# A decoder of two layers on one core: one skip term, the front stage's last rounds, the token list of the experts, and the first three heads' keys

## The reference, cut to what matters

```python
x = LN(x + diff_attention(x))                 # front stage
x = LN(x + long_conv(v=x, x1=ctx, x2=ctx))    # conv stage, middle stage
x = LN(x + moe(x))                            # 8 experts, 2 for each token
x = LN(x + attention(x))                      # tail: "P"
x = LN(x + cross_attention(x, ctx))           # tail: "C"
x = LN(x + shared_kv_attention(x))            # tail: "H" and "A"

# long_conv: kv = v_i * x2_j in groups of 8 rows (i, j in the group)
y = conv(kv, filter) + kv * skip;  out_j = sum_i y_ij * x1_i
# moe: top 2 of 8 logits, each token goes to two experts
# shared_kv_attention, 16 heads of 32:
gating = softmax(x @ W_gate.T);  idx = argmax(gating)
k_shared = one_hot(idx) . k      # one head's keys for each token
v_shared = one_hot(idx) * max(gating) . v
```

## Time and profile before

| | |
|---|---|
| median of 3 runs | 2275.7 us (2269.55 to 2280.37) |
| the profiled execution's own time, its span | 2275.38 us, 2273.6 us |
| granted TensorE clock, mean | 0.966 |
| PE busy, DVE busy | 2116.7 us (93%), 1231.6 us (54%) |
| ACT busy, POOL busy | 517.4 us (23%), 589.0 us (26%) |
| on the chain that ended last | PE 37%, DVE 5%, ACT 1%, POOL 1% of the span |

### The profile page before, as it was taken

How to read it: one execution, slowest core, us unless ns; L and a number is a source line. 1 busy time by engine, 2 the same in 40 slices (tenths; PEclk the granted TensorE clock), 3 DMA queues, 4 the chain that set the end, 5 groups by cost and what they waited for, 6 DMA issues and landing times. The chain is left out here.

```text
span 2273.6 us, 29273 instructions
## 1 busy us (share of the span) xinstructions
PE 2116.7 (93%) x11864; PEld 1231.1 (54%) x11872; DVE 1231.6 (54%) x1861; ACT 517.4 (23%) x783; POOL 589.0 (26%) x544
## 2 busy tenths in 40 slices
PE   6899999888999899799999878999999999999996
PEld 4444444233444476456666646566666666666653
DVE  2467777667999841022222234355757575747456
ACT  1444444430000121111111112122222222222221
POOL 1122222227888405011110311212121212111112
PEclk9999999989999899899999989999999999999997
DMA  9840000005111146811221510101010101000000
GB/s 174 96 40 29 29 29 19 31 19 191 41 46 41 51 152 113 230 65 66 67 67 61 205 69 29 47 1 47 1 56 1 57 1 38 3 27 10 1 10 19
DMA packets 66762, 129.63 MB, mean 57 GB/s; under 512 B 7450, under 2 KB 20968, under 8 KB 66632
## 3 DMA queue, kind: packets, MB, share of 16 engines
q1 hardware_dynamic: 44952, 75.43, 13.1%
q10 hardware_dynamic: 14976, 33.69, 5.3%
q0 software_dynamic: 6704, 18.64, 2.8%
HBM read 96.38 MB, written 41.85 MB: 61 GB/s over the span
## 5 line engine op out<-in xcount | busy, mean ns | idle before, releaser
L925 PE MATMUL conv_conv<-kv,toep 128*128 128x512 f32 x576 | 248.9, 595 | 4.6 <-POOL kv L946 4.6
L2223 DVE RECIPROCAL tail_inv<-tail_ring 128x256 f32<-128x256 f32 x64 | 112.4, 1756 | 181.6 <-PE tail_ring L1691 181.4
L1393 PE MATMUL moe_gu_ps<-gu,moe_xT 128*128 x624 | 199.6, 463 | 3.4 <-issue 1.8
L925 PEld LDWEIGHTS conv_conv<-kv,toep 128*128 128x128 f32 x576 | 110.0, 191 | 144.2 <-issue 136.1
L946 POOL TENSOR_TENSOR kv<-vT,cT 128x512 f32<-128x512 f32 x128 | 160.5, 1275 | 48.7 <-PE conv_conv L925 38.9
L1393 PEld LDWEIGHTS moe_gu_ps<-gu,moe_xT 128*128 128x128 f32 x624 | 116.3, 192 | 72.8 <-issue 23.6
L1968 POOL TENSOR_TENSOR tail_rstd_x<-tail_rstd_x,const_minus_half 128x2 f32<-128x2 f32 x32 | 22.6, 707 | 482.1 <-DVE tail_rstd_x L2175 482.1
L1975 POOL TENSOR_SCALAR_AFFINE_SELECT tail_expT<-tail_expT 128x1024 f32<-128x1024 f32 x64 | 70.4, 1100 | 288.6 <-ACT tail_expT L2045 288.1
L540 POOL TENSOR_SCALAR_AFFINE_SELECT front_expT<-front_expT 128x2048 f32<-128x2048 f32 x32 | 64.4, 2012 | 259.8 <-ACT front_expT L598 259.8
L1475 DVE TENSOR_TENSOR moe_hid<-moe_gu_ps,moe_silu 128x352 f32<-128x352 f32 x39 | 20.5, 525 | 179.4 <-PE moe_gu_ps L1393 179.4
L2045 ACT ACTIVATE tail_expT<-tail_scores 128x1536 f32<-128x1536 f32 x64 | 92.8, 1451 | 76.4 <-PE tail_scores L1669 76.4
(11 more groups left out here) (335 smaller groups left out, 4035.7 us busy)
## 6 DMA issues: line engine op xcount, KB each, us to landing
toep<-toeplitz SPq DMA_DIRECT2D x32, 320.0 KB, 2.8
y_slots<-moe_y ACTq DMA_DIRECT2D x39, 256.0 KB, 2.0
gu<-in_L_ffn_gate_up_proj SPq DMA_DIRECT2D x5, 1408.0 KB, 10.5
toeplitz<-filt_rows SPq DMA_DIRECT2D x1, 6144.0 KB, 67.2
front_e<-in_ctx SPq DMA_DIRECT2D x8, 512.0 KB, 5.6
toeplitz<-filt_rows SPq DMA_DIRECT2D x2, 2048.0 KB, 89.9
x_after<-x SPq DMA_DIRECT2D x8, 512.0 KB, 5.1
tail_x<-x_after SPq DMA_DIRECT2D x8, 512.0 KB, 3.8
```

What stands on the lines that cost most here:

```text
L925: ins = pe.matmul(bank, toep[p][:, mat * P:(mat + 1) * P], kv[p][:, c].rearrange("p b j i -> p (b j i)"), start=n == 0, stop=n == len(PART ...
L1393: ins = pe.matmul(gu_ps[:, s % 2, h, 0:HID], xT[:, c, :], wgu[c][:, e, h * HID:(h + 1) * HID], start=c == 0, stop=c == NC - 1)
L2223: link.after(dve.reciprocal(inv[c % 2][:], bank[:, S:2 * S]))
```

## The change

- **Skip term of the last sequence.** In the front stage, `skip_products(7)` writes into the buffer `e[2]`, which is free by then, and that stage ends after it, without `octets(7)`, `add_skip(7)` and the store of batch 7. These become the first work of the conv stage on PE, DVE and SP. The wait for `base_stored` stays where it was on ACT.
- **Order of the front stage's end.** In round 10, PE takes `turn_context(7)`, `weigh(7, 1, 1)` and `square_sums(7, 0)` ahead of `turn_tokens(6)`; ACT takes the context, the sums and the root ahead of the tokens.
- **One-hot token list.** DVE makes, for each token's two slots, a one-hot row of its lane in the tile (`at_lane`, 128 wide, bf16) and its tile marked with the row number and the block number (`marked`, 2 x 39, bf16). 32 bf16 matmuls sum them into one bank; DVE adds block * 128 + row. They stand after b = 2 of the context loop. The 32 indirect DMAs, the clearing of `token_of`, its load and its transpose go. SP issues the second half of the weights when the bank is filled.
- **End of the middle stage.** The wait for `ctx_q` and `ctx_o` moves from ACT's end of the middle stage to the top of ACT's list in the experts stage, ahead of the load of `wq`.
- **Gates with three heads' keys.** `wgate` and `gk` lie side by side in one tensor. The gates' products have 16 + 96 = 112 columns (for both t), the keys' products 416 columns instead of 512. `gate_choice` copies 2 x 112 columns out of PSUM instead of 2 x 16; `pick("k")` is two products instead of one: 96 columns from SBUF and 416 from PSUM. `wgate` is loaded with the other H weights, later than before.

```diff
@@ front stage, PE
                     elif f is not None:
-                        turn_tokens(u)
                         turn_context(f)
                         weigh(f, 1, 1)
                         square_sums(f, 0)
+                        turn_tokens(u)
                         square_sums(f, 1)
                         octets(u)
...
                     elif u is not None:
                         turn_tokens(u)
-                        octets(u)
@@ front stage, SP and DVE
-                for b in range(B):
+                for b in range(B - 1):
                     sp.wait_ge(based, b + 1)
...
-                    if u is not None: skip_products(u)
+                    if u is not None: skip_products(u, skipped if u < B - 1 else e[last_skip])
...
-                    if u is not None: add_skip(u)
+                    if u is not None and u < B - 1: add_skip(u)
@@ conv stage, PE, SP, DVE: ahead of their loops
+                for t in range(NT):
+                    bank = ring.claim(pe, ("oct", t))
+                    pe.matmul(bank, consts["octets"][:], skipped[:, t, :], start=True, stop=True).then_inc(ring.filled_sem(("oct", t)), 1)
...
+                sp.wait_ge(based, 1)
+                sp.dma_start(base.rearrange("(b t p) d -> b p t d", p=P, t=NT)[B - 1], x_last).then_inc(mid.base_stored[(B - 1) % 5], 16)
...
+                for t in range(NT):
+                    key = ("oct", t)
+                    dve.wait_ge(ring.filled_sem(key), ring.count(key))
+                    dve.tensor_tensor(skipped[:, t, :], ring.tile(key), e_last[:, t, :], ALU.mult).then_inc(ring.drained_sem(key), 1)
...
+                dve.tensor_tensor(x_last, x_last, skipped[:], ALU.add).then_inc(based, 1)
@@ middle stage, PE
                 for b in range(1, B - 2):
                     ctx_queries(b)
                     ctx_values(b)
-                pe.wait_ge(rows_loaded, 16)
-                bank = ring.claim(pe, "tokens")
-                pe.transpose(bank[:, 0:TILES], token_rows[:], consts["ident"][0:TILES, 0:TILES]).then_inc(ring.filled_sem("tokens"), 1)
+                    if b == 2:
+                        pe.wait_ge(hot_ready, 1)
+                        bank = ring.claim(pe, "tokens")
+                        for t in range(T):
+                            for n in range(PICKS):
+                                ins = pe.matmul(bank[:, 0:2 * TILES], at_lane[:, t, n], marked[:, t, n].rearrange("p a s -> p (a s)"),
+                                                start=t + n == 0, stop=t + n == T + PICKS - 2)
+                        ins.then_inc(ring.filled_sem("tokens"), 1)
@@ middle stage, SP and POOL
-                sp.wait_ge(placed, 16 * T * PICKS)
-                sp.dma_start(token_rows[:], token_of.rearrange("(a p) o -> a (p o)", p=P)).then_inc(rows_loaded, 16)
+                sp.wait_ge(ring.filled_sem("tokens"), ring.count("tokens"))
...
-                for t in range(T):
-                    for n in range(PICKS):
-                        pool.indirect_dma_start(
-                            out=token_of, out_offset=bass.IndirectOffsetOnAxis(ap=slot[:, t, n:n + 1], axis=0),
-                            in_=ids[:, t:t + 1], in_offset=None).then_inc(placed, 16)
@@ middle stage, DVE, behind tile_expert
+                dve.wait_ge(stored[NX - 1], 16 * len(range(NX - 1, B, NX)))
+                link.after(dve.tensor_tensor(reached[:], over(slot_f[:], TILES + 1), over_picks(bounds[:], TILES + 1), ALU.is_ge))
+                link.after(dve.tensor_reduce(tile_of[:], reached[:, :, :, 1:TILES + 1], AX_X, ALU.add))
+                link.after(dve.scalar_tensor_tensor(out=lane_of[:], in0=tile_of[:], scalar=-float(P), in1=slot_f[:], op0=ALU.mult, op1=ALU.add))
+                dve.tensor_tensor(at_lane[:], over(lane_of[:], P), over_picks(lanes[:], P), ALU.is_equal)
+                link.after(dve.tensor_tensor(in_tile[:], reached[:, :, :, 0:TILES], reached[:, :, :, 1:TILES + 1], ALU.subtract))
+                dve.tensor_scalar(marked[:, :, :, 0], in_tile[:], row_id[:, 0:1], None, ALU.mult)
+                dve.tensor_tensor(marked[:, :, :, 1], in_tile[:], block_id[:].unsqueeze(2).unsqueeze(3).to_broadcast([P, T, PICKS, TILES]),
+                                  ALU.mult).then_inc(hot_ready, 1)
@@ ACT: end of the middle stage, top of the experts stage
-                for p in range(2):
-                    act.wait_ge(ctx_stored[p], 32 * ((B - 2) // 2))
...
+                for p in range(2):
+                    act.wait_ge(mid.ctx_stored[p], 32 * ((B - 2) // 2))
                 for k in early:
@@ tail, PE (the eight calls of rows("H", "k", ...) become shared_keys)
+                    n = NG + LED * HD
+                    for t in range(NT):
+                        ins = project_rows(pe, bank[:, t * n:(t + 1) * n], xT[b % 2], t, wide["gk"], 0, n)
...
+                def shared_keys(b, t):
+                    bank = ring.claim(pe, ("H", "k", b, t))
+                    project_rows(pe, bank[:, 0:D - LED * HD], xT[b % 2], t, wide["gk"], NG + LED * HD,
+                                 NG + D).then_inc(ring.filled_sem(("H", "k", b, t)), 1)
@@ tail, DVE, pick("k")
-                        ins = dve.tensor_tensor(chosen, bank, of, ALU.mult)
+                        dve.tensor_tensor(chosen[:, 0:LED], led[:, t].rearrange("p (h d) -> p h d", d=HD), of(0, LED), ALU.mult)
+                        ins = dve.tensor_tensor(chosen[:, LED:NG], bank[:, 0:NG - LED], of(LED, NG), ALU.mult)
```

More of the change, by code:

```diff
@@ L632, in _ @@
                             take(("turn", d, n), pair(xT, n))
-                    if a is None and u is not None:
-                        for n in range(2):
-                            take(("x1", u, n), vT[:, 2 * n:2 * n + 2, u, :])
                     if a is None and f is not None:
@@ L640, in _ @@
                     if f is not None: root(f, 0)
+                    if a is None and u is not None:
+                        for n in range(2):
+                            take(("x1", u, n), vT[:, 2 * n:2 * n + 2, u, :])
                     if d is not None: take_query(d, 0)
@@ L856, in __init__ @@
         self.base_stored = [st.sem(f"base_stored{p}") for p in range(5)]
+        self.ctx_stored = [st.sem(f"ctx_stored{p}") for p in range(2)]
         self.gathered = [st.sem(f"gathered{p}") for p in range(2)]
@@ L967, in _ @@
                 link = Link(dve, linked, 1 << 30)
+                for t in range(NT):
[3 more added lines that the diff above has]
+                for t in range(NT):
+                    key = ("oct", t)
+                    dve.wait_ge(ring.drained_sem(key), ring.count(key))
+                dve.tensor_tensor(x_last, x_last, skipped[:], ALU.add).then_inc(based, 1)
                 def sums(h, lc):
@@ L986, in _, with middle_stage @@
                         sums(h, lc)
-def middle_stage(nc, consts, mid, region, base, x_out, vT, cT, w_router, w_gu, w_down, wa, wvo, ctx_q, ctx_o, token_of, slot, share):
+def middle_stage(nc, consts, mid, region, base, x_out, vT, cT, w_router, w_gu, w_down, wa, wvo, ctx_q, ctx_o, slot, share):
     T = B * NT
@@ L1037, in middle_stage @@
         stored = [st.sem(f"stored{p}") for p in range(NX)]
-        ctx_stored = [st.sem(f"ctx_stored{p}") for p in range(2)]
         router_loaded = st.sem("router_loaded")
@@ L1536, in tail_stage @@
         descending = st.sb("descending", [P, NG])
-        gate, gex, ranked, ind = (st.sb(n, [P, NT, NG]) for n in ("gate", "gex", "ranked", "ind"))
+        gated = allowed[:, 2, 0:NT * (NG + LED * HD)].rearrange("p (t n) -> p t n", t=NT)
+        gate, led = gated[:, :, 0:NG], gated[:, :, NG:NG + LED * HD]
+        gex, ranked, ind = (st.sb(n, [P, NT, NG]) for n in ("gex", "ranked", "ind"))
         gtop, first, gsum, gval = (st.sb(n, [P, NT]) for n in ("gtop", "first", "gsum", "gval"))
@@ L1813, in _ @@
                     if A_: shared_out(a)
-                    if H_: turned("H", h); rows("H", "k", h, 0, xT[h % 2], wide["gk"]); gates(h)
+                    if H_: turned("H", h); shared_keys(h, 0); gates(h)
                     if r == 0:
@@ L1848, in _ @@
                 score("A", a, 1)
-                rows("H", "k", h, 0, xT[h % 2], wide["gk"])
+                shared_keys(h, 0)
                 score("A", a, 2)
@@ L1854, in _ @@
                 rows("C", "v", c, 1, xT[c % 2], wvo)
-                rows("H", "k", h, 1, xT[h % 2], wide["gk"])
+                shared_keys(h, 1)
                 shift("A", a)
@@ L1927, in _ @@
                 load("wo")
-                load("wgate")
                 for b in range(2):
@@ L1933, in _ @@
                 sp.wait_ge(ring.filled_sem(key), ring.count(key))
-                for k in ("gk", "gv", "gq"):
+                for k in ("wgate", "gk", "gv", "gq"):
                     load(k)
@@ L2237, in gate_choice @@
                     key = ("H", "g", b)
```

(9 more changed lines are left out.)

89 lines of the change are left out of this document (50 added, 39 removed).

## The result

| | before | after |
|---|---|---|
| median of the runs, us | 2275.5 (2269.55 to 2280.37, n = 4) | 2248.94 (2246.92 to 2251.49, n = 4) |
| ratio, 95% interval | | 0.9881 [0.9859, 0.9902] |
| profiled execution, us (span) | 2275.38 (2273.6) | 2249.93 (2248.1) |

Forecast 2256.5 (2247 to 2266), measured 2248.94: 26.6 us saved where the working found 19.2. The time lies in the range, outside the likeliest case's own 2251 to 2261. The issues that open the stages say where the two profiled spans part. Each column is the length of a stretch in us, ended by the row named.

What follows compares the result with a forecast made beforehand. It took TensorE alone to pace the tail, and TensorE and VectorE both to be full in conv. Savings of 1.5 + 8.2 + 9.5 = 19.2 us from the median of 2275.7 gave 2256.5 us, range 2247 to 2266.

Steps and rivals of the forecast that it cites:

- likeliest case: Whole kernel: the forecast as it stands, 15 to 24 us saved, so 2251 to 2261 us; chance 0.68.
- Front, order of round 10: End of the front stage: weigh starts 2.8 us sooner, ACT's token copies give 1.2 back; about 1.5 us saved.
- Seam to conv: Front to conv: the stage starts 5.1 us sooner, but its first both comes 5.1 us later from there.
- this lasts to the end: Conv stage: the 5.1 us delay of the first both stays, since DVE's following 243 us are full.
- Rival 1: Conv stage: the late store costs more, PE gets no free bank, 7.8 us more delay, 2264 us; chance 0.12.
- Rival 2: Conv stage: DVE catches up as L985 waits less, 4.5 us more saved, 2252 us; chance 0.10.
- rival 4: Conv stage: POOL locks L985 at its dear end, 28 us added, 2284 us, slower than before; chance 0.04.
- Middle: End of the middle stage: the experts start at 934.5 instead of 942.68, 8.2 us saved.
- SP's weights are gone by 910 or so: Middle stage: SP's second half of the weights starts at about 891 and is gone by 910 or so.
- Tail: Tail: shorter key products save 1.26 us a sequence, six rounds 7.5 and the last two sequences 2.0; 9.5 us saved.
- Rival 3: Tail: the gates' 112 columns come on top of the weight loads, the key change does nothing, 2266 us; chance 0.06.
- The lock that the prediction weighed: Tail picks: with two SBUF inputs a pick may wait for one POOL instruction, 0.9 us; the sum stays.

Runs made afterwards that it cites:

- e2: The kernel before with the new order of round 10 alone (token turns and copies moved later); 2292.73 us, ratio 0.9996 to the kernel before.
- e1: The kernel before with the skip term of batch 7 made in the conv stage, nothing else; 2291.3 us, ratio 0.9991 to the kernel before.
- e3: The kernel before with the one-hot token list and the moved wait for the context stores alone; 2267.48 us, ratio 0.9883 to the kernel before.
- e6: The changed kernel with ACT's waits for the stores of base, its x loads and first gu load moved behind its copy for h = 3; 2245.35 us.
- e10: The changed kernel with 14 unused products of 512 columns added behind PE's last product of the conv stage; 2254.43 us.
- e4: The kernel before with the gates' 96 shared key columns alone; 2284.25 us, ratio 0.9955 to the kernel before.
- e8: The changed kernel with ACT's wait for the context stores back at the end of the middle stage, the one-hot list kept; 2256.06 us.
- e7: The changed kernel with four heads' keys in the gates' products (144 columns) instead of three (112); 2247.17 us.
- e9: The changed kernel with all 512 key columns multiplied again, the gates still 112 columns wide and their 96 key columns unused; 2257.71 us.
- e12: The changed kernel with e6's late loads, e7's four heads, and batch 7's octets, their DVE work and store of base behind h = 0 of conv; 2249.06 us.

## Why the prediction was nearly right, point by point

**Front, order of round 10: 1.5 forecast, 2.9 measured** (e2, and e1 against the kernels with both). Its two steps were right: `weigh` starts 2.6 us sooner (forecast 2.8), and ACT's token copies give 0.9 back (1.2), since from the first square sum to the second it is now 6.08 us instead of 5.13. At one clock in `weigh` that makes 1.6 us at the second square sum, e2 against e3. Missing is the clock, 1.3 us in `weigh`; the forecast priced this stretch at one level.

**Seam to conv: 5.1 saved, 5.1 lost; measured 5.4 saved and 6.1 lost.** The mechanism was right as far as `both`: the store of `base` and ACT's wait for it, for e6 without the wait has `both` 8.4 us behind the start. Three sizes were off, and they nearly cancel, which is luck. The landing took 9.2 us for 4 to 5, the loads behind it 2.0 for 3.7, so `both` came 8.5 us later than before and not 5.1. And "this lasts to the end" was wrong by 2.4 us, which DVE made up (next point). Rival 1 didn't come: PE ran its 576 products without a gap, in 248.6 us (before 248.9). Rival 2 came in part, 2.4 of its 4.5 us, by its own mechanism.

**L985's spread, rival 4.** It didn't decide, but it is real. The line's mean was 1168 ns before, 1131 after, and 1113 to 1144 in six of the others and 804 to 825 in six, never in between:

```profile
L1001 DVE TENSOR_TENSOR prod<-total,cT x64: 692/882/1514, 533.6 to 772.2; 128x512 f32<-128x512 f32 x64
```

```profile
L1002 DVE TENSOR_TENSOR prod<-total,cT x64: 691/693/1611, 527.2 to 769.2; 128x512 f32<-128x512 f32 x64
```

(One line's ns, min/median/max, first of the changed kernel, then of e6.) In windows 640:680 DVE is busy 38.93 us of 40 in the first state and 36.08 in the second. In the first, dear state DVE sets the stage's end. From its first `total` to SP's load of `wr` it takes 243.88 us before and 241.49 after; without the line's own 64 products (74.8 and 72.4 us) that is 169.1 in both, and in five more of the eight profiles in that state (all but e10, whose added products end its stage). So the late `both` goes through to the end, less what the line gives: 8.5 us late, 2.4 given back, 6.1 longer. In the second, cheap state PE sets the end: in all six profiles the stage ends 2.8 to 2.9 us behind its last product.

No run has the late `both` in the cheap state. By estimate it would cost nothing there, since 169.1 + 52.8 = 222 us of DVE's work would fit behind it; and an early `both` in the dear state would end at 10.1 + 241.5 = 251.6 us, before PE's 255. e6 changed both at once, so its 3 to 5 us may be put down to either. In the kernel before the dear state cost 1.1 us: 254.05, and 252.98 in e4, with the cheap one, the same code in this stage and the same 248.9 us of PE's stream.

The Trainium skill, "SBUF — State Buffer", "Who interferes with whom", names what may be the reason, a shared port pair that VectorE and GpSimd lock against each other. The rows fit it, but no run took GpSimd's work away. That there are two states, and nothing between, is what these rows add; what chooses the state is open.

**Middle: 8.2 forecast, 9.0 measured.** The one-hot products took 1.34 us instead of 2.0, and nothing else was off in size. The reasons were mixed, though. "SP's weights are gone by 910 or so" is nearly right of the loads issued by 891, which land by 913, but one load waits for the last context values and goes at 926. The moved wait carries 6.7 of the 9.0 (e8), the list 2.3. In the group of e1 to e4 the list carries some 17 more (25.9 for the whole edit).

**Tail: 9.5 forecast, 11.9 measured.** Rounds: 1.26 forecast, 1.21 measured, as priced by the line through two widths; a third width (e7) and the free columns (e9: 0.08 us) agree. Rival 3 is out. The missing term is the clock: the last two sequences gave 5.1 us instead of 2.0, some 2.6 of it the clock by the estimate above. Behind wide gates the key product took 3.06 instead of 4.57 us, where its 96 columns fewer are worth 0.6. The lock that the prediction weighed against this change shows in 2 of 16 picks: the new product of 96 columns with both inputs in SBUF took 251 to 260 ns fourteen times and 1066 and 1266 ns twice, so it was no term of the sum.

**Chance.** 2.7 us at the middle's start came by no edit.

Added up for the profiled pair: front and seam 0.7 more than forecast (8.3 - 6.1 = 2.2 against 1.5), middle 0.8, its clock 2.7, tail 2.4, less 0.2 in the experts: 6.4 us on top of 19.2, and 25.6 stands beside the spans' 25.5. The medians lie 26.6 apart; the last microsecond is within their spread.

What stays open: what the scatters of four-byte rows block in one group of runs and not in another, and whether they alone explain why the kernel before takes 2299 us in the third group, where no profile has them; what puts L985 in one state or the other; and why one of four kernels with the old order kept its clock in round 10.

## What to carry to other kernels

Where TensorE's weight loads set the pace, columns added to those products are nearly free up to the load's time (0.08 us for 96 columns in 16 gates), and shorten another product at full price (1.2 us a round): look for narrow products that share their weights with a wide one. A wait that only protects a later reader belongs behind the first work that doesn't need it: here two waits of ACT, for stores in DRAM, were worth 6.7 us of a stretch (the context stores, moved by the change) and 3 to 5 us of a stage, 2.6 by the medians (the store of `base`, which the change made late; DVE's state changed with it). And a list made by tiny scattered writes should be timed on more than one chip and occasion.

## What the runs showed of the hardware that was not expected

- 32 scatters of 128 four-byte rows left PE untouched in one profile (96.05 us for the stretch) and went with one starved by some 17 us in three others (112.7 to 113.5): the kernel before took 2275.5, 2278.16, 2293.35 and 2299.29 us in four groups of runs, the changed one 2248.94 and 2247.94 in the two in which it ran.
- Sixteen products of 16 and of 112 columns take nearly the same at 1.2 GHz, 3.56 and 3.73 us. Behind the same idle time of 2.2 us, PE ran the key product after the narrow ones at 1.2 GHz in four profiles of four, and after the wide ones at 2.4 GHz in nine of nine (the tenth was at 2.4 GHz all through).
- One VectorE product beside GpSimd has two means over a stage, 804 to 825 and 1113 to 1168 ns, and nothing between them in fourteen profiles. In the dear state VectorE set the stage's end, in the cheap one TensorE did.
- A store of 512 KB landed in 2.7 us behind the weight loads (e12) and in 7.8 to 9.3 us beside them.
